# Routing stages of a four-layer gated cross-attention kernel moved and shortened, and the key exponentials of its linear attention taken from PSUM on ScalarE

## What is computed

```python
x = x + tanh(g_xattn[0]) * attention_16_heads(layernorm(x), ctx)      # masked
x = x + tanh(g_ffn[0])   * moe_top1(layernorm(x))    # 16 experts, capacity 256
x = x + tanh(g_xattn[1]) * attention_16_heads(layernorm(x), ctx)      # + side biases
x = x + tanh(g_ffn[1])   * ternary_ffn(layernorm(x))
x = x + tanh(g_xattn[2]) * attention_1_head(layernorm(x), ctx)        # relu projections
x = x + tanh(g_ffn[2])   * moe_top2(layernorm(x))    # 8 experts, no capacity
x = x + tanh(g_xattn[3]) * linear_attention_8_heads(layernorm(x), ctx)
x = x + tanh(g_ffn[3])   * moe_top2(layernorm(x))    # 8 experts, with a capacity
```

## Time and profile before

| | us |
|---|---|
| median of 3 executions | 1773.62 |
| lowest, highest | 1773.33, 1784.85 |
| the profiled execution | 1773.25 |
| its span (first to last instruction) | 1771.5 |
| PE, PE weight loads busy | 1287.9, 1040.0 |
| DVE, ACT, POOL busy | 1053.3, 679.8, 744.0 |

### The profile page before, as it was taken

One profiled execution on the slowest core, in us unless ns is written; L12 is line 12 of the kernel. 1 busy time (PEld: TensorE's weight loads), 2 busy tenths in 40 slices (PEclk: granted clock), 3 DMA queues, 4 the chain that ended last, 5 costly groups with the idle time before them and its releaser, 6 DMA issues. The chain is left out here.

```text
span 1771.5 us, 36736 instructions
## 1 busy us (share of the span) xinstructions
PE 1287.9 (73%) x11964; PEld 1040.0 (59%) x11964; DVE 1053.3 (59%) x3181; ACT 679.8 (38%) x1574; POOL 744.0 (42%) x914
## 2 busy tenths in 40 slices
PE   3888884927888698785499920688888764999980
PEld 2676773926666465474388820466656554888860
DVE  3777762247887666686122249588998951444435
ACT  2755550416886243341144410245444421222220
POOL 1335453526775111656344410354666652333330
PEclk9988875967999799765699965799999966999995
DMA  4222202624331000111477740100000002222205
GB/s 126 102 89 70 84 14 71 209 70 133 105 107 50 12 0 13 53 38 57 135 203 210 208 125 8 30 1 2 14 17 14 17 31 79 72 63 75 61 27 142
DMA packets 155862, 129.97 MB, mean 73 GB/s; under 512 B 21162, under 2 KB 133564, under 8 KB 155712
## 3 DMA queue, kind: packets, MB, share of 16 engines
q1 hardware_dynamic: 144448, 106.98, 21.1%
q0 software_dynamic: 11264, 21.07, 3.5%
HBM read 89.77 MB, written 40.57 MB: 74 GB/s over the span
## 5 line engine op out<-in xcount | busy, mean ns | idle before, releaser
L1495 POOL DMA_INDIRECT l_rows_out<-l3e_y,l3e_target x80 | 77.7, 971 | 175.8 <-DVE l3e_y L1482 155.9
L1449 ACT ACTIVATE l3e_sT<-l3e_ps_h 128x256 f32<-128x256 f32 x160 | 61.5, 384 | 177.6 <-PE l3e_ps_h L1419 149.8
L1468 DVE TENSOR_TENSOR l3e_hT<-l3e_sT,l3e_ps_h 128x256 f32<-128x256 f32 x160 | 67.4, 421 | 98.9 <-ACT l3e_sT L1449 98.9
L1495 POOL DMA_INDIRECT l_rows_out<-l2e_y,l2e_target x80 | 77.7, 971 | 104.7 <-DVE l2e_y L1480 66.6
L1446 ACT ACTIVATE l2e_hT<-l2e_ps_h,l2e_b 128x256 f32<-128x256 f32 x160 | 69.9, 474 | 98.3 <-PE l2e_ps_h L1414 98.3
L1418 PE MATMUL l3e_ps_h<-l3e_xT,l3e_w 128*128 128x256 f32 x320 | 100.7, 396 | 4.9 <-DVE l3e_xT L1459 0.6
L1419 PE MATMUL l3e_ps_h<-l3e_xT,l3e_w 128*128 128x256 f32 x320 | 96.1, 382 | 0.0
L958 POOL DMA_INDIRECT l_rows_in<-l2a_rt_rows,l2f_slot x64 | 62.6, 978 | 51.1 <-DVE l2f_slot L946 30.9
L1428 PE MATMUL l2e_ps_y<-l2e_w,l2e_hT 128*128 128x128 f32 x640 | 79.2, 277 | 0.0
L1428 PE MATMUL l3e_ps_y<-l3e_w,l3e_hT 128*128 128x128 f32 x640 | 78.0, 275 | 0.0
L1414 PE MATMUL l2e_ps_h<-l2e_xT,l2e_w 128*128 128x256 f32 x320 | 77.6, 386 | 0.6 <-DVE l2e_xT L1459 0.6
(11 more groups left out here) (543 smaller groups left out, 3833.5 us busy)
## 6 DMA issues: line engine op xcount, KB each, us to landing
l2e_w<-in_L_ffn_w SPq DMA_DIRECT2D x80, 256.0 KB
l1a_side<-in_fside_Bx16xSxS SPq DMA_DIRECT2D x32, 512.0 KB, 3.7
...
```

Source lines behind the costliest of these rows:

```text
L1449: nc.scalar.activation(sT[:, f % 2, :], ps_h[f % 2][:, 0:CHUNK], act_func).then_inc(s_ready, 1)
L1468: nc.vector.tensor_tensor(hT[:, b, f, :], sT[:, f % 2, :], ps_h[2 + f % 2][:, 0:CHUNK], ALU.mult).then_inc(h_ready, 1)
L1495: pool.indirect_dma_start(out=r.rows_out, out_offset=bass.IndirectOffsetOnAxis(ap=target[:, c % 2, a:a + 1], axis=0), in_=y[:, c % 2, a, : ...
```

## The change

- **Count.** `count` goes. `running`, four vectors per quad, holds the count ahead of each tile (with the expert's first row already in it); the new `prefix` makes the next four by four chained additions of 128x16 or 128x8. It runs on POOL in layers 0 and 3, on DVE in layer 2. `positions` is two matmuls: triangular times `member`, ones times `running`. `slots` no longer adds the base (5 operations for 6; without a capacity 3 for 4). With one pick the copy to `member` goes.
- **Layer 0.** Each stage from `turn` on is one or two steps later; logits and positions stand behind `values(i+1)` and write the second half of the bank of `turn_p`, so `turn_p`'s second half now waits until DVE has read them. `summed(i-1)` stands ahead of `maximum(i+2)`, `residual(i)` behind it (layer 1's attention too).
- **Layer 2.** `turn`, `turned`, `logits`, `read`, `choose`, `prefix`, `positions` and `slots` all work on quad `i-1`, `normalise` on quad `i`: two steps earlier at the end. The loop is one step shorter. Scatters go tile by tile.
- **Layer 3.** `kc` goes. ACT takes the key exponentials from `ps_kv` itself, in eight activations of 128x64 (one for each head, the head's negative maximum as bias), and one of 128x8; PE's `values` waits for all nine. The routing stages are two steps earlier, the loop two steps shorter; the 17 operations of `statistics` on DVE are replaced by `bn_aggr` for each tile, three operations on POOL and one on DVE; `normalise` takes a quad at once.
- A function `route` that nothing called is removed.

The core of the diff (the removed function, renumbered waits of the same kind, `prepare` and buffers are left out):

```diff
@@ attention16
-        ps_l = ps_b[:, 18 * HALF:18 * HALF + 64]
+        ps_l = ps_t[:, 4:8, :].rearrange("p j k -> p (j k)")
@@ attention16, pool
+                    router.prefix(pool, quad(i - 5))
                     router.statistics_on_pool(pool, quad(i - 1), s["summed"])
                     router.normalise_on_pool(pool, quad(i - 1))
-                    router.scatter_tile(pool, i - 9)
+                    router.scatter_tile(pool, i - 11)
@@ attention16, turn_p
                 if routing is not None and half == 0:
-                    reused(pe, router.s["turned_ready"], (t - 3) // 4)
+                    reused(pe, router.s["turned_ready"], (t - 4) // 4)
+                if routing is not None and half == 1:
+                    reused(pe, router.s["lg_read"], (t - 5) // 4)
+                    reused(pe, router.s["pos_read"], (t - 7) // 4)
@@ attention16, tensor
                 turn_p(i + 1, 0)
-                if routing is not None:
-                    route_scores(i)
                 output(i)
                 turn_p(i + 1, 1)
                 project(i + 4, i + 2)
                 values(i + 1)
                 if routing is not None:
-                    router.turn(pe, quad(i - 2), turned_tile)
+                    router.logits(pe, quad(i - 4), ps_l)
+                    router.positions(pe, quad(i - 6), ps_l)
...
+                    router.turn(pe, quad(i - 3), turned_tile)
@@ attention16, vector
                 outputs(i)
                 masked(i + 2)
+                if routing is not None:
+                    router.read(dve, quad(i - 5), ps_l)
+                summed(i - 1)
+                maximum(i + 2)
                 residual(i)
                 if routing is not None:
-                    router.read(dve, quad(i - 4), ps_l)
-                    router.slots(dve, quad(i - 5), ps_l)
-                maximum(i + 2)
-                summed(i)
+                    router.slots(dve, quad(i - 7), ps_l)
                 centred(i + 2)
                 if routing is not None:
-                    router.choose(dve, quad(i - 4))
-                    router.count(dve, quad(i - 4))
+                    router.choose(dve, quad(i - 5))
@@ Router
+    def prefix(self, eng, q):
...
+            eng.tensor_tensor(out, self.running[:, q % 2, j, :], self.members(q)[:, j, :], ALU.add).then_inc(s["running_ready"], 1)
@@ Router.positions
-        for j in range(Q - 1):
-            self.nc.tensor.matmul(out[:, j + 1:Q, :], self.ones[:, :], member[:, j:j + 1, :].broadcast_to([P, Q - 1 - j, E]),
-                                  start=False, stop=False)
-        self.nc.tensor.matmul(out, self.ones[:, :], self.seen[:, q % 2, :].unsqueeze(1).broadcast_to([P, Q, E]),
-                              start=False, stop=True).then_inc(s["pos_ps"], 1)
+        pe.wait_ge(s["running_ready"], Q * q + Q)
+        self.nc.tensor.matmul(out, self.ones[:, :], self.running[:, q % 2, 0:Q, :], start=False, stop=True).then_inc(s["pos_ps"], 1)
@@ attention1, tensor
                 scores(i + 1)
+                router.turn(pe, i - 1, ps_r)
                 project_context(i + 3)
                 turn_p(i)
                 turn_x(i + 2)
-                router.positions(pe, i - 3, ps_l[:, 256:512])
+                router.logits(pe, i - 1, ps_l)
                 values(i)
                 project(i + 2)
-                router.logits(pe, i - 2, ps_l)
-                router.turn(pe, i - 1, ps_r)
+                router.positions(pe, i - 1, ps_l[:, 256:512])
@@ attention1, vector
-                router.slots(dve, i - 3, ps_l[:, 256:512])
+                router.read(dve, i - 1, ps_l)
                 residual(i)
+                router.choose(dve, i - 1)
+                router.prefix(dve, i - 1)
                 router.statistics(dve, i, s["summed"])
-                router.read(dve, i - 2, ps_l)
-                router.choose(dve, i - 2)
-                router.count(dve, i - 2)
+                router.slots(dve, i - 1, ps_l[:, 256:512])
@@ linear_attention, values on tensor
-                pe.wait_ge(s["kc_ready"], 2 * t + 1)
+                pe.wait_ge(s["ek_ready"], (H + 1) * (t + 1))
@@ linear_attention, key_exponents on scalar
-                nc.scalar.activation(ek[:, :], kc[:, :], ACT.Exp).then_inc(s["ek_ready"], 1)
+                for c in range(H):
+                    at = slice(c * S, (c + 1) * S)
+                    nc.scalar.activation(ek[:, at], ps_kv[:, at], ACT.Exp, bias=nmk[:, c:c + 1]).then_inc(s["ek_ready"], 1)
+                nc.scalar.activation(ek[:, I:I + H], nmk[:, :], ACT.Exp, bias=nk[:, :]).then_inc(s["ek_ready"], 1)
@@ linear_attention, vector
-                router.read(dve, quad(i - 6), ps_l)
-                router.slots(dve, quad(i - 7), ps_l)
+                router.read(dve, quad(i - 4), ps_l)
+                router.slots(dve, quad(i - 5), ps_l)
                 key_denominators(i + 2)
                 summed(i - 1)
-                router.statistics(dve, quad(i - 1), s["summed"])
-                router.choose(dve, quad(i - 6))
-                router.count(dve, quad(i - 6))
+                router.choose(dve, quad(i - 4))
+                router.aggregate(dve, i - 1, s["summed"])
+                router.offsets(dve, quad(i - 2))
```

432 lines of the change are left out of this document (117 added, 315 removed).

## The result

| | before | changed |
|---|---|---|
| median of 20 executions | 1773.99 us | 1781.86 us |
| lowest, highest | 1768.75, 1784.85 | 1774.30, 1788.99 |
| the profiled execution's span | 1771.5 | 1781.1 |

The ratio is 1.0046, with a 95% interval of 1.003 to 1.0062: 8 us slower, within 1%. The forecast was 1778, the likeliest case "within 1%".

A forecast was written before the change was run, and what follows sets the result against it. Bounds were taken by phase: layer 0 DVE's score loop plus routing, layer 2 a nearly always busy DVE, layer 3 the key chain plus routing. Layers 0, 2 and 3: −21 + 22 + 3 = +4 on 1773.25, 1778 us, range 1752 to 1803.

The forecast's parts named there:

- Layer 2: Layer 2's attention: lost overlap makes steps 15.4 to 19.5 us, the end gives time back; +22 us, between +8 and +34.
- My circle: Layer 2: statistics, normalise, turn, logits, values, residual, choose and prefix form one loop without overlap, 15.4 to 19.5 us a step.
- my sign: Layer 2: PE's turn would have an idle of about 8 us or more ahead, ending on ACT's rt_rows.
- Layer 0: Layer 0's attention: less routing in DVE's and PE's steps, less a new bank wait; −21 us, between −28 and −6.
- bank wait: Layer 0: turn_p's second half waits until DVE has read the positions in the shared bank, 2.2 us a quad.
- quads near 25 instead of 29: Layer 0: sign that the forecast is right, routed quads taking near 25 us instead of 29.
- Layer 3: Layer 3's attention: dearer exponentials against cheaper routing; +3 us, between −26 and +25, with −15 to +20 kept in the range.
- exponentials: Layer 3: nine activations take 2.0 us, so ACT's value copy comes 1.05 us later in 31 steps, +32.5 us.
- The half clock in layer 2: Rival: half clock through layer 2 and in layer 0's bank waits; +31, 1805 us, chance 0.22.
- the cheap exponentials: Rival in layer 3: the nine take 1.1 us, or the next step doesn't wait for the value copy; 1749 us, chance 0.12.
- the full clock: Rival: full clock in both layer 0 and layer 2; −17, 1756 us, chance 0.12.
- The layer 3 rival: Rival: layer 3's routing still costs 3 us more a quad, against the longer key chain; +19 more, 1797 us, chance 0.12.

The follow-up runs named there:

- e4: The changed kernel with layer 2 in the order of the kernel before, new routing stages kept; ratio 0.9903 to the kernel before, layer 2 346.3 us.
- e3: The changed kernel with layer 2's statistics moved ahead of choose and prefix on DVE; ratio 1.0065 to the kernel before, layer 2 388.9 us.
- e6: The changed kernel with layers 0 and 1's attention in the old order and bank, shortened stages kept; ratio 1.0103 to the kernel before, layer 0 351.2 us.
- e7: The changed kernel with layer 0's logits and positions in the attention output's bank, read and slots heading DVE's step; ratio 0.9947 to the kernel before, layer 0 327.6 us.
- e2: The changed kernel with kc on DVE and one 520-column exponential again in layer 3; ratio 0.9902 to the kernel before, layer 3 614.0 us.
- e1: The kernel before with only layer 3's nine key exponentials added; ratio 1.0084 to the kernel before, layer 3 655.4 us.

## Why the prediction was right, point by point

- **The sum** came out at +4, measured +8 (ratio) and +9.6 between the two profiled spans. The parts were off by up to 11 us, and the errors had both signs, so the sum is nearer than its terms. That is luck in part.
- **Layer 2**, +22 forecast, +19.6 measured. The loop grew by 35.9 (forecast 40, between 27 and 52), the end gave 12.8 (forecast 17 to 19), and the start 3.5, which I had not looked for; e4 has these 3.5 too, so they come with the shortened stages or `prepare`, and which one wasn't tried. The step lies between the values for the two clock levels (16.0 to 17.0 between 15.4 and 19.5), nearer the higher clock than I took. My circle went through the statistics alone; e3 shows that the positions close it as well, and there my sign failed: the turn's idle was to be about 8 us and is 2.67, because 3.81 come ahead of the positions.
- **Layer 0**, −21 forecast, −10.1 between the two profiles (16 to 20 on the first occasion): the weakest term. Its loop gave 17.6 of the 23 that I took, and start and end took back 7.5 where I had 2. My reason for the gain, the move of positions away from the output, holds: e6 against e7 gives the moves about 24 us. The bank wait came as forecast, 2.2 us, and with the clock it costs 20.8 us of the loop (171.4 − 150.6, e7), where my sum has 21 (14 for the wait, 7 for the clock). What was too small is the rest: without the bank wait I left 2.4 us of routing in each quad, 15 to 16 in all, and e7's loop is still 20.9 us longer than 26 quiet steps (150.6 − 129.7). Of the sign "quads near 25 instead of 29" little is seen: they took 26.2 to 29.7, and 9.5 of the loop's 17.6 us come in the last one (28.8 to 19.3).
- **Layer 3**, +3 forecast, +2.9 measured, with both terms a fifth too large: exponentials +27.4 for +32.5, routing −24.5 for −30 (split by e2; by e1 it is +16.9 and −14.0). That the errors cancel is luck. The step of 9.0 and the 1.94 us were right, and the quads took 36.6 to 37.0 for the most part, forecast near 38. What I had not seen is where the cost falls: 14.4 in the loop, where the routed quads hide part of it, and 11.5 in four steps of start-up, 5 of them as longer waits and the rest, it seems, through the clock.
- **Rivals.** The half clock in layer 2 came only in its last steps (1.27 and 1.14 us for logits and values up to 780, 2.05 for the values from 795 on); the cheap exponentials did not come (1.94, not 1.1); the full clock came in neither phase. The layer 3 rival did not come either: the routing gave 5.5 us less than forecast, not 19 less.
